# A graph network over a dense 2708 x 2708 matrix: later adj passes and the W2 product by seven products in place of eight

## The chip, the cores and the metric

The kernel runs on 1 core of one Trainium2 chip. The metric is device time in microseconds, the median of several runs, lower is better. TensorE multiplies, VectorE (DVE), ScalarE (ACT) and GpSimd (POOL) work on tiles, SyncE (SP) issues DMAs.

## The reference

x is 2708 x 512, adj 2708 x 2708 (about 2% of its entries are not zero, but it is treated as dense), W1 512 x 1024, W2 1024 x 1024, W3 1024 x 512, all float32. The inputs are drawn in the test; the function is

```python
def _gc(x, adj, W, b):
    return adj @ (x @ W) + b
h = jnp.maximum(_layernorm(x, axis=-1), 0.0)
h = jax.nn.relu(_gc(h, adj, W1, b1))
h = jax.nn.relu(_gc(h, adj, W2, b2))
return x + _gc(h, adj, W3, b3)
```

(the last three lines are `_L0_gnn_ref`, here written into one). The layer norm has eps 1e-5 and no weights.

## The kernel before, in words

**Order of the products.** The kernel forms adj times a matrix in four passes, each with 512 columns of the matrix as stationary operand: `pass1` = adj (normed x); `h1a`, `h1b` = the two halves of relu(pass1 W1 + b1), each followed by its pass, `pass2a` and `pass2b`; `w2` = relu(W2 product + b2); `w3` = its product with W3; `pass3` = adj (that) + b3 + x. 2708 = 21 blocks of 128 and a tail of 20.

**Float32 in three.** Each operand is cut in two fp32r parts, hi (ACT, L530, a CAST) and lo = value - hi (DVE, L551, a subtraction with two SBUF inputs), and `three` (L867 to L869) multiplies hi hi, hi lo and lo hi into one PSUM bank. The tail of 20 rows lies three times in one tile of 84 partitions and needs one matmul (L891).

**A pass.** The 2708 columns go in six chunks of 4, 4, 4, 4, 3 and 2 blocks (512, 384 and 276 wide). For each chunk 21 tiles of adj, 128 x width, are loaded (L419, `raw`, RAW = 7 buffers), cut into a ring (`slot_hi`, `slot_lo`, RING = 7), and each is the moving operand of 4 banks x 3 matmuls. The stationary operand, `still_hi` and `still_lo` of 21 x 512, stays in SBUF. Results are drained by DVE (L806, L816, L813 in pass 3) into `P1` in SBUF or into `stage` (STAGES = 4), and ACT issues their stores (L652 for the output), waiting for DVE's drain. `P2` and `H2` are in DRAM. In all 8352 matmuls: 5920 of 512 columns, 1216 of 384 and 1216 of 276, by the loops.

**The first chunk of pass 1.** Beside each adj tile comes a tile of x (`stage`, loaded by L402 after the tile four before it is cut). DVE takes its statistics two tiles ahead (L712, L714), POOL computes with columns of 128 x 1 (L833 to L847), ACT takes the root and centres (L673, L678) and writes hi (L506), DVE lo (L543). DVE's order for tile n is `statistics(n + 2)`, `inverse(n + 1)` (L719), the cut of the adj tile, the cut of the x tile.

**Order of waits.** Every engine has one list of steps. A load waits until the `raw` buffer's last tile is cut by DVE; a cut by ACT waits for the load and for the ring slot's last matmul; TensorE waits for DVE's `lo_done`. POOL has no work after the x tiles. SP only loads.

## Time and profile before

| what | us |
|---|---|
| median of 3 runs (1734.08 to 1735.21) | 1734.35 |
| the profiled execution: span | 1732.1 |
| TensorE busy (99%), 8352 matmuls | 1717.0 |
| DVE busy (36%) | 628.4 |
| ACT busy (26%) | 451.6 |
| POOL busy (3%) | 43.8 |
| moved by DMA | 190.17 MB, 110 GB/s |

The span runs from the first to the last instruction of one execution; the difference to the median is what lies around it. Matmuls are pipelined: a busy TensorE is one that always has a matmul in it, and the mean of one (0.39 us at 512 columns) is longer than the step from one start to the next. The granted clock was at full speed (2.4 GHz) in all forty slices of the page.

### The profile page before, as it was taken

The page shows a single profiled execution, that of the slowest core. Times are in us where ns is not written, and L with a number is a line of the kernel's source. Part 1 is how long each engine was busy: PE and PEld are TensorE (multiplying, and loading weights), DVE is VectorE, ACT ScalarE, POOL GpSimd, SP SyncE. Part 2 cuts the span into 40 slices and gives each one's busy share as a digit, 9 for nine tenths or more (in the row PEclk, how much of TensorE's full clock was granted, in tenths as well). Part 3 has the DMA queues.
Part 4 walks back from the last instruction along what each step waited for, and adds up shares of the span by engine and source line. Part 5 has one row for each costly group of instructions (what it writes and reads, how often), then busy time and mean ns, then how long its engine had stood idle before and what let it go on. Part 6 is the DMA issues. An engine that isn't in the chain of part 4 may idle for free.

```text
span 1732.1 us, 23105 instructions
## 1 busy us (share of the span) xinstructions
PE 1717.0 (99%) x8352; PEld 1480.0 (85%) x8352; DVE 628.4 (36%) x1040; ACT 451.6 (26%) x829; POOL 43.8 (3%) x115
## 2 busy tenths in 40 slices
PE   7999999999999999999999999999999999999999
PEld 6788889988888899888888899888898888888899
DVE  7623333463332333653233353222233332333232
ACT  6522222332221222332222242111012322222221
POOL 6400000000000000000000000000000000000000
PEclk9999999999999999999999999999999999999999
DMA  5633333024443342133344365332253324444342
GB/s 187 190 94 102 97 97 83 9 62 119 124 116 105 107 128 70 32 105 113 108 121 120 100 188 146 95 96 85 84 154 106 98 87 136 143 147 122 105 123 86
DMA packets 133485, 190.17 MB, mean 110 GB/s; under 512 B 14938, under 2 KB 64698, under 8 KB 133422
## 3 DMA queue, kind: packets, MB, share of 16 engines
q1 hardware_dynamic: 99450, 161.39, 32.5%
q10 hardware_dynamic: 33972, 27.98, 4.9%
q8 instruction: 34, 0.56, 0.1%
q14 instruction: 29, 0.24, 0.0%
HBM read 161.34 MB, written 27.73 MB: 109 GB/s over the span
## 4 chain that ended last, share of the span: by engine, by line
PE 96%; DMA 1%; DVE 1%; POOL 1%; ACT 1%; issue 0%; ACTq 0%; DVEq 0%; SPq 0%
PE ps L867 32%; PE ps L868 32%; PE ps L869 32%; DMA stage<-x 1%; PE ps L891 1%; DVE stats L712 0%; DVE still_lo L543 0%; POOL spread L835 0%; POOL spread L833 0%; POOL spread L843 0%; DVE slot_lo L551 0%; ACT stage L678 0%; ACT still_hi L506 0%; ACT slot_hi L530 0%; DVE moments L714 0%
## 5 line engine op out<-in xcount | busy, mean ns | idle before, releaser
L867 PE MATMUL ps<-slot_hi,still_hi 128*128 128x512 f32 (+2 forms) x2016 | 735.1, 365 | 11.4 <-DVE still_lo L543 11.4
L868 PE MATMUL ps<-slot_lo,still_hi 128*128 128x512 f32 (+2 forms) x2016 | 734.3, 364 | 0.0
L869 PE MATMUL ps<-slot_hi,still_lo 128*128 128x512 f32 (+2 forms) x2016 | 734.0, 364 | 0.0
L551 DVE TENSOR_TENSOR slot_lo<-raw,slot_hi 128x512 fp32r<-128x512 f32 (+2 forms) x588 | 362.8, 631 | 752.0 <-ACT slot_hi L530 751.5
L530 ACT CAST slot_hi<-raw 128x512 fp32r<-128x512 f32 (+2 forms) x588 | 328.5, 573 | 1056.5 <-PE ps L869 784.1
L867 PEld LDWEIGHTS ps<-slot_hi,still_hi 128*128 128x128 f32 x2016 | 379.8, 188 | 65.4 <-DVE still_lo L543 12.4
L868 PEld LDWEIGHTS ps<-slot_lo,still_hi 128*128 128x128 f32 x2016 | 379.9, 188 | 53.0
L869 PEld LDWEIGHTS ps<-slot_hi,still_lo 128*128 128x128 f32 x2016 | 379.6, 188 | 53.1
L867 PE MATMUL ps<-W_hi,slot_hi 128*128 128x512 f32 x336 | 132.1, 393 | 0.0
L868 PE MATMUL ps<-W_lo,slot_hi 128*128 128x512 f32 x336 | 132.1, 393 | 0.0
L869 PE MATMUL ps<-W_hi,slot_lo 128*128 128x512 f32 x336 | 132.1, 393 | 0.0
L867 PE MATMUL ps<-slot_hi,W_hi 128*128 128x512 f32 (+2 forms) x336 | 122.1, 363 | 0.0
L868 PE MATMUL ps<-slot_lo,W_hi 128*128 128x512 f32 (+2 forms) x336 | 121.9, 363 | 0.0
L869 PE MATMUL ps<-slot_hi,W_lo 128*128 128x512 f32 (+2 forms) x336 | 121.9, 363 | 0.0
L868 PEld LDWEIGHTS ps<-W_lo,slot_hi 128*128 128x128 f32 x336 | 63.3, 188 | 14.0
L869 PEld LDWEIGHTS ps<-W_hi,slot_lo 128*128 128x128 f32 x336 | 63.3, 188 | 14.0
L867 PEld LDWEIGHTS ps<-W_hi,slot_hi 128*128 128x128 f32 x336 | 63.3, 188 | 13.7
L868 PEld LDWEIGHTS ps<-slot_lo,W_hi 128*128 128x128 f32 x336 | 63.1, 188 | 8.8
L869 PEld LDWEIGHTS ps<-slot_hi,W_lo 128*128 128x128 f32 x336 | 63.1, 188 | 8.7
L867 PEld LDWEIGHTS ps<-slot_hi,W_hi 128*128 128x128 f32 x336 | 63.1, 188 | 8.7
L808 DVE TENSOR_SCALAR stage<-ps,b_cols 128x512 f32<-128x512 f32 (+2 forms) x48 | 32.7, 687 | 76.9 <-PE ps L869 72.8
L816 DVE COPY stage<-ps 128x512 f32<-128x512 f32 (+2 forms) x48 | 30.1, 628 | 60.0 <-PE ps L891 60.0
(63 smaller groups left out, 563.4 us busy)
## 6 DMA issues: line engine op xcount, KB each, us to landing
raw<-adjT SPq DMA_DIRECT2D x336, 256.0 KB, 2.7
raw<-adjT SPq DMA_DIRECT2D x84, 192.0 KB, 2.4
raw<-adjT SPq DMA_DIRECT2D x84, 138.0 KB, 2.1
raw<-H SPq DMA_DIRECT2D x42, 256.0 KB, 2.9
raw<-W SPq DMA_DIRECT2D x32, 256.0 KB, 3.1
P<-stage ACTq DMA_DIRECT2D x32, 256.0 KB, 2.1
raw<-P SPq DMA_DIRECT2D x32, 256.0 KB, 2.7
H<-stage ACTq DMA_DIRECT2D x32, 256.0 KB, 2.3
```

What stands on the lines that cost most here:

```text
L530: act.copy(hi, src).then_inc(hi_done, 1)
L551: dve.tensor_tensor(lo, src, hi.bitcast(F32), ALU.subtract).then_inc(lo_done, 1)
L808: dve.tensor_scalar(stage[:, d.stage, 0:w], ps[:, d.bank, 0:w], b2_cols[:, d.part:d.part + 1], 0.0, ALU.add, ALU.max).then_inc(drained, 1)
L816: dve.tensor_copy(stage[:, d.stage, 0:w], ps[:, d.bank, 0:w]).then_inc(drained, 1)
L867: pe.matmul(out, st_hi, mv_hi, start=start, stop=False)
L868: pe.matmul(out, st_hi, mv_lo, start=False, stop=False)
L869: return pe.matmul(out, st_lo, mv_hi, start=False, stop=stop)
L891: return pe.matmul(out, still_tail[0:REP, b * P:(b + 1) * P], slot_tail[0:REP, 0:w], start=False, stop=True)
```

## The change

**Seven products.** In `pass2a`, `pass2b`, `pass3` and `w2` the operands are seen as 2 x 2 blocks: adj by pairs of row blocks (t, t + 10), t = 0 to 9, and by two halves of 1356 columns (adj's columns are padded from 2708 to NP = 2712); the stationary operand by the same pairs and by two halves of its 512 columns. Seven products X_i Y_i take the place of eight: three of blocks as they are, four of sums and differences. Row block 20 and the tail are added directly, to the groups of parts 1, None, 5 and 6. Each half goes in CHUNKS = 3 chunks of W = 452 columns. A group is one part of one chunk: 10 tiles of adj (or of its combinations), each for 2 banks x 3 matmuls; in `w2` 4 tiles, each for 4 banks x 3. Its drain adds it to partial results in SBUF (`parts`, `e(i)`); part 4 is added in two places.

**The combinations of adj** are made once, in pass 1, by POOL (`make`: four subtractions of 452 columns for each pair and chunk) from the loaded tiles, and stored to `TS`, from which the later passes load. Those of the stationary operands are made in `combine` (POOL, for pass 2a and pass 3) or in `prep_stationary` (POOL, from `H1B` and `W2` in DRAM, with DMAs issued by POOL), stored, and loaded and cut anew in groups 2, 3, 5, 6 and 7 of the last chunk of pass 2a and pass 2b (ten or eight tiles of 128 x 256 among the ten moving tiles) and in the first two groups that follow. `prep_moving` does the same for the moving operand of `w2`.

**Pass 1** stays direct, but with 3 chunks of 2 x 452 columns, eight banks and adj tiles of 904 columns, RAW1 = 5, RING1 = 3. x tiles have XS = 3 buffers. The results `P1` go to DRAM. W1 is done in one phase `h1` with both halves; its first half stays in SBUF, the second (`H1B`) goes to DRAM.

**Stores.** ACT issued them after waiting for the drain. Now SP does, in its stream of loads: the store of parts 1, 4, 5 and 6 stands two tiles behind the drain (`later(2, store)`; four in pass 3), the drain LAG = 5 tiles behind its group. RAW and RING are 5. In pass 3 POOL adds x (`finish`), with its own loads of `xT`.

```diff
-RING = 7
-RAW = 7
-HEAD = 4
-LATE = 4
-STAGES = 4
...
-CHUNK_BLOCKS = (4, 4, 4, 4, 3, 2)
...
+ORDER = (1, 2, 3, 4, 5, 6, 0, 7, 8, 9)
+EARLY = 8
+BLOCKS = [b for t in ORDER for b in (t, t + PAIRS)] + [20, SHORT]
...
+W = 452
+CHUNKS = 3
+HALF = W * CHUNKS
+NP = 2 * HALF
...
+DIRECT = {0: (0, 0), 1: (1, 0), 6: (1, 1)}
+X11, X12, S2, S3, S1, X22, S4 = range(7)
+
+RING = 5
+RAW = 5
+RAW1 = 5
+RING1 = 3
+XS = 3
+LAG = 5
...
+    def adj_pass(name, late, reload=None, ahead=(), own=()):
+        last_of = {}
+        ahead, own = list(ahead), list(own)
+        for c in range(CHUNKS):
+            for g_n, part in enumerate((0, 1, 2, 3, None, 4, 5, 6)):
...
+                half = {1: 0, None: 1, 5: 0, 6: 1}.get(part)
+                for t in here + ([20] if half is not None else []):
+                    if t == 20:
+                        j = p.tile("left", True)
+                        j.chunk, j.half = c, half
+                        g.left = j
+                        p.release(j, g, True)
...
+                    if half is not None and (t == here[0] if here else True):
+                        p.tails += 1
+                        g.tail = (p.tails, c, half, at["tail_freed"])
+                        at["tail_freed"] = g.done[-1]
+                        p.steps.append(("tail", g))
+                    spread_in(extra)
+                    if late:
+                        late.pop(0)()
+                    if own and c == 0 and g_n == 0 and len(g.tiles) > RING + 1:
+                        own.pop(0)()
+                    p.emit_due()
...
+                p.later(LAG, lambda g=g: drain_product(g))
...
+    def drain_product(g):
+        part = g.part
+        count_drains(g, (0, 1), 2 if part == 4 else 1)
+        finals = {1: ("c11", 4), 4: ("c22", 6), 5: ("y", 2), 6: ("x", 0)}.get(part)
+        needs = {0: 0, 1: 4, 3: 2, None: 6}.get(part)
+        busy = [p.busy(("e", needs + m)) for m in range(2)] if needs is not None else [None, None]
+        p.steps.append(("drain", (g, p.copied if part == 0 else p.drained, busy)))
+        if finals:
+            p.owed |= {("e", finals[1] + m) for m in range(2)}
+            def store():
+                for m in range(2):
+                    p.store(("e", finals[1] + m))
+                p.steps.append(("store", (g, finals, g.free_drained)))
+                if g.phase != "pass3":
+                    at["p2", g.phase, g.chunk] = dict(p.stored)
+            if g.phase == "pass3":
+                p.final += 2
+                p.final_of[g.chunk, g.part] = p.final
+                p.steps.append(("finish", (g, finals, g.free_drained, p.final)))
+                p.later(4, store)
+            else:
+                p.later(2, store)
...
+                if n >= XS:
+                    sp.wait_ge(lo1_done, xs1[n - XS].ready)
+                sp.dma_start(xs[:, n % XS, :], x[b * P:(b + 1) * P, :]).then_inc(x_in[n % XS], 16)
...
+                elif j.kind == "moving" and j.part in DIRECT:
+                    k, a = DIRECT[j.part]
+                    b = j.pair + k * PAIRS
+                    col = a * HALF + j.chunk * W
+                    sp.dma_start(raw[:, r, 0:W], adjT[b * P:(b + 1) * P, col:col + W]).then_inc(raw_in[r], 16)
+                elif j.kind == "moving":
+                    if "made" not in seen:
+                        seen["made"] = 1
+                        for i in range(2):
+                            sp.wait_ge(made_stored[i], 16 * made_total // 2)
+                    k = (j.part - 2) * W
+                    sp.dma_start(raw[:, r, 0:W], TS[j.pair, j.chunk, :, k:k + W]).then_inc(raw_in[r], 16)
...
+                elif kind == "store":
+                    g, finals, number = a
+                    half = 0 if g.part in (1, 5) else 1
+                    side = 0 if g.part in (1, 6) else 1
+                    col = half * HALF + g.chunk * W
+                    if g.phase == "pass3":
+                        sp.wait_ge(finished, plan.final_of[g.chunk, g.part])
+                    else:
+                        sp.wait_ge(drained, number)
...
+                elif kind == "tail":
+                    n = a.tail[0]
+                    act.wait_ge(tail_in, 48 * n)
+                    act.wait_ge(group_done, a.tail[3])
+                    act.copy(slot_tail[0:REP, 0, :], raw_tail[0:REP, 0, :]).then_inc(tail_hi, 1)
...
+            def make(i, which):
+                c, n = divmod(i, PAIRS)
+                a, b = chunks1[c][2 * n], chunks1[c][2 * n + 1]
+                upper, lower = raw1[:, a.raw % RAW1, :], raw1[:, b.raw % RAW1, :]
+                Y11, Y12, Y21, Y22 = upper[:, 0:W], upper[:, W:2 * W], lower[:, 0:W], lower[:, W:2 * W]
+                T2_, T3_, T1_, T4_ = (made[:, i % 2, k, :] for k in range(4))
+                if which == 0:
+                    if i >= 2:
+                        pool.wait_ge(made_stored[i % 2], 16 * (i // 2))
+                    pool.wait_ge(raw1_in[a.raw % RAW1], 16 * (a.raw // RAW1 + 1))
+                    pool.tensor_tensor(T1_, Y12, Y11, ALU.subtract).then_inc(made_done, 1)
+                    pool.wait_ge(raw1_in[b.raw % RAW1], 16 * (b.raw // RAW1 + 1))
+                    pool.tensor_tensor(T3_, Y22, Y12, ALU.subtract).then_inc(made_done, 1)
+                else:
+                    pool.wait_ge(made_done, 4 * i + 1)
+                    pool.tensor_tensor(T2_, Y22, T1_, ALU.subtract).then_inc(made_done, 1)
+                    pool.wait_ge(made_done, 4 * i + 3)
+                    pool.tensor_tensor(T4_, Y21, T2_, ALU.subtract).then_inc(made_done, 1)
+
...
+            def prep_moving(c, q):
+                cols = [slice(a * HALF + c * W, a * HALF + (c + 1) * W) for a in range(2)]
+                y11, y12, y21, y22 = (prep[:, i, 0:W] for i in range(4))
+                for i, (k, a) in enumerate(((q, 0), (q, 1), (KF + q, 0), (KF + q, 1))):
+                    prep_load(i, P2[k, :, cols[a]], prep[:, i, 0:W])
+                n = state["done"]
+                state["done"] += 4
+                pool.wait_ge(prep_in[0], state["in"][0])
+                pool.wait_ge(prep_in[1], state["in"][1])
+                pool.tensor_tensor(y11, y12, y11, ALU.subtract).then_inc(prep_done, 1)
+                pool.wait_ge(prep_in[3], state["in"][3])
+                pool.tensor_tensor(y12, y22, y12, ALU.subtract).then_inc(prep_done, 1)
+                pool.wait_ge(prep_done, n + 2)
+                prep_store(0, T2[0, q, c, :, :], y11)
+                prep_store(1, T2[1, q, c, :, :], y12)
+                pool.tensor_tensor(y22, y22, y11, ALU.subtract).then_inc(prep_done, 1)
+                pool.wait_ge(prep_in[2], state["in"][2])
+                pool.wait_ge(prep_done, n + 3)
+                pool.tensor_tensor(y21, y21, y22, ALU.subtract).then_inc(prep_done, 1)
+                pool.wait_ge(prep_done, n + 4)
+                prep_store(2, T2[2, q, c, :, :], y22)
+                prep_store(3, T2[3, q, c, :, :], y21)
...
+            def product_group(g):
+                first = g.chunk == 0 and g.phase in ("pass2a", "pass3")
+                phase = "h1" if g.phase == "pass2a" else "w3"
+                side = 0 if g.part in (0, 1, 6) else 1
+                for n, j in enumerate(g.tiles):
+                    if first:
+                        pe.wait_ge(stat_lo, plan.stat_of[phase, j.pair, j.part])
+                    pe.wait_ge(lo_done, j.cut + 1)
+                    s = j.slot % RING
+                    for m in range(2):
+                        cols = slice(m * P, (m + 1) * P)
+                        if n == 0:
+                            bank_free(g, m)
+                        end = g.left is None and n == len(g.tiles) - 1
+                        mm = three(ps[:, g.banks[m], 0:W], S[:, j.pair, j.part, 0, cols], S[:, j.pair, j.part, 1, cols],
+                                   ring[:, s, 0, 0:W], ring[:, s, 1, 0:W], start=n == 0, stop=end)
+                        if end:
+                            mm.then_inc(group_done, 1)
+                    if not end:
+                        mm.then_inc(slot_used, 1)
```

## Rows read from the trace of the kernel before

**Rows 1.** The profile's page: busy time by engine; below, the chain by line.

```profile
PE 1717.0 (99%) x8352; PEld 1480.0 (85%) x8352; DVE 628.4 (36%) x1040; ACT 451.6 (26%) x829; POOL 43.8 (3%) x115
...
PE ps L867 32%; PE ps L868 32%; PE ps L869 32%; DMA stage<-x 1%; PE ps L891 1%; DVE stats L712 0%; DVE still_lo L543 0%; POOL spread L835 0%; POOL spread L833 0%; POOL spread L843 0%; DVE slot_lo L551 0%; ACT stage L678 0%; ACT still_hi L50
```

**Rows 2.** Waits of TensorE: us in total, times, longest.

```profile
PE ps L867 <- DVE still_lo L543: 11.4, 3, 9.5
```

**Rows 3.** Timeline of TensorE, 512 columns: start, us, operation; 18 rows left out.

```profile
399.63 0.39 PE L869 MATMUL ps<-slot_hi,still_lo 128*128 128x512 f32 x1
...
403.93 0.39 PE L867 MATMUL ps<-slot_hi,still_hi 128*128 128x512 f32 x1
```

**Rows 4.** The same, 384 columns; 12 rows left out.

```profile
254.71 0.33 PE L869 MATMUL ps<-slot_hi,still_lo 128*128 128x384 f32 x1
...
256.96 0.33 PE L867 MATMUL ps<-slot_hi,still_hi 128*128 128x384 f32 x1
```

**Rows 5.** The same, 276 columns; 14 rows left out.

```profile
299.83 0.29 PE L867 MATMUL ps<-slot_hi,still_hi 128*128 128x276 f32 x1
...
301.76 0.29 PE L867 MATMUL ps<-slot_hi,still_hi 128*128 128x276 f32 x1
```

**Rows 6.** Groups by line and form: count, busy us, mean ns of one, idle before.

```profile
L551 DVE TENSOR_TENSOR slot_lo<-raw,slot_hi 128x512 fp32r<-128x512 f32 x406 | 273.2, 689 | 545.5 <-ACT slot_hi L530 545.2 <-DVE still_tail L745 0.2
L530 ACT CAST slot_hi<-raw 128x512 fp32r<-128x512 f32 x406 | 244.8, 620 | 740.7 <-PE ps L869 561.4 <-DVE stage L808 67.2 <-DVE stage L816 65.6
...
L551 DVE TENSOR_TENSOR slot_lo<-raw,slot_hi 128x276 fp32r<-128x276 f32 x91 | 39.6, 445 | 94.3 <-ACT slot_hi L530 94.3
L530 ACT CAST slot_hi<-raw 128x276 fp32r<-128x276 f32 x91 | 37.6, 423 | 140.3 <-PE ps L869 100.0 <-DVE stage L808 17.4 <-DVE stage L816 15.1
```

**Rows 7.** Timeline of the first 11 us, all engines.

```profile
0.73 0.53 POOL L850 MEMSET slot_tail<- 128x512 f32 x1 [0.29 <-POOLq L1035]
...
5.74 0.34 POOL L843 TENSOR_SCALAR spread<-spread 128x1 f32<-128x1 f32 x1 [0.54 <-DVE spread L719]
...
9.53 0.79 PE L867 MATMUL ps<-slot_hi,still_hi 128*128 128x512 f32 x1 [9.53 <-DVE still_lo L543]
...
9.87 0.43 SPq L419 DMA_DIRECT2D raw<-adjT  x1
...
10.12 0.63 PE L868 MATMUL ps<-slot_lo,still_hi 128*128 128x512 f32 x1
...
10.54 0.63 PE L869 MATMUL ps<-slot_hi,still_lo 128*128 128x512 f32 x1
```

**Rows 8.** The chain of waits from 38 to 62 us: start, us, what.

```profile
46.66 2.65 DMA stage<-x
...
49.34 0.70 DVE stats L712
...
50.06 0.19 DVE moments L714
...
61.08 1.37 POOL spread L843
```

**Rows 9.** Timeline around 46 us, DVE and POOL.

```profile
42.52 0.13 DVE L719 RECIPROCAL spread<-spread 128x1 f32<-128x1 f32 x1
...
45.88 0.75 DVE L543 SCALAR_TENSOR_TENSOR still_lo<-stage,spread,still_hi 128x512 fp32r<-128x512 f32 x1 [0.15 <-ACT still_hi L506]
...
46.07 0.77 POOL L843 TENSOR_SCALAR spread<-spread 128x1 f32<-128x1 f32 x1
```

**Rows 10.** DMA issues: count, KB each, median us from issue to landing.

```profile
raw<-adjT SPq DMA_DIRECT2D x336, 256.0 KB, 2.7
...
raw<-adjT SPq DMA_DIRECT2D x84, 138.0 KB, 2.1
```

**Rows 11.** One stretch of 2 us: PE, PEld, DVE, ACT, POOL busy, clock, DMA share, GB/s.

```profile
1000.00:1002.00 2.00, 2.00 (x14) 2.00 (x13) 1.44 (x3) 1.51 (x3) 0.00 (x0) 1.00 1.06 396
```

**Rows 12.** Timeline of the last matmul.

```profile
1728.96 0.29 PE L891 MATMUL ps<-slot_tail,still_tail 84*128 84x276 f32 x1
```

More of the change, by code:

```diff
@@ L37 @@
 BANK = 512
[L38 to L67 removed]
+EPS = 1e-5
+STEP = 32
+PAIRS = 10
+FULL = 21
+SHORT = 21
+ORDER = (1, 2, 3, 4, 5, 6, 0, 7, 8, 9)
+EARLY = 8
@@ new lines, with __init__ @@
+BLOCKS = [b for t in ORDER for b in (t, t + PAIRS)] + [20, SHORT]
[11 more added lines that the diff above has]
+LAG = 5
+class Tile:
+    def __init__(self, kind, cut):
+        self.kind, self.cut = kind, cut
+        self.raw = self.raw_freed = self.slot = None
+        self.block = self.part = self.pair = self.chunk = self.half = self.k = None
+        self.freed = self.place_freed = None
@@ L68, in __init__, with columns_chunk @@
+def columns_chunk(block):
+    first = block * P
+    last = min(first + P, 2 * HALF) - 1
+    return max((c % HALF) // W for c in range(first, last + 1))
+class Pass1Tile:
+    def __init__(self, kind, cut):
         self.kind, self.cut, self.ready = kind, cut, cut + 1
-        self.chunk, self.tile, self.col, self.width, self.half, self.source = chunk, tile, col, width, half, source
-        self.raw = self.raw_freed = self.tail_use = self.slot = self.acc_before = self.slot_before = None
+        self.raw = self.raw_freed = self.pair_freed = self.slot = None
+        self.freed = self.place_freed = None
+        self.chunk = self.block = self.n = self.k = self.col = None
@@ L367, in source_of @@
[L367 to L383 removed]
+        copied = sem("copied")
@@ L818, in finish @@
-            def finish(dve, g, i):
-                if g[0].phase != "w3":
-                    still_lo_part(g, len(g[0].drains) - 1, i)
-                    dve.wait_ge(still_done, count([u.drains[-1].still for u in g], i))
-            run_cuts_and_drains(dve, cut, drain, finish, drain_first=("h1a", "h1b"))
+                    elif n + 2 <= SHORT:
+                        statistics(n + 2)
+                    if n + 1 <= SHORT:
+                        inverse(n + 1)
+                dve.wait_ge(hi1_done, j.cut + 1)
@@ new lines, in w2_group @@
+            def w2_group(g):
+                for n, j in enumerate(g.tiles):
+                    pe.wait_ge(lo_done, j.cut + 1)
+                    s = j.slot % RING
+                    for m in range(4):
+                        half, mm_col = divmod(m, 2)
+                        cols = slice(mm_col * P, (mm_col + 1) * P)
+                        if n == 0:
+                            bank_free(g, m)
+                        t = 2 * j.pair + half
+                        mm = three(ps[:, g.banks[m], 0:W], S[:, t, j.part, 0, cols], S[:, t, j.part, 1, cols],
+                                   ring[:, s, 0, 0:W], ring[:, s, 1, 0:W], start=n == 0, stop=n == 3)
+                        if n == 3:
+                            mm.then_inc(group_done, 1)
+                    if n < 3:
+                        mm.then_inc(slot_used, 1)
```

1857 lines of the change are left out of this document (1138 added, 719 removed).

## The prediction

> **What bounds the kernel now.** I read the busy times first: TensorE 1717.0 of 1732.1 us, and 32% of the chain that ended last for each of the three lines of `three`, 96% in all [rows 1]. The waits of TensorE come next: 11.4 us on its first line, of which 9.53 are the start [rows 2, 7]. So nothing but the stream of matmuls sets the end, and time is gained by fewer or narrower ones. The timeline gives the price of one, start to start. 512 columns: 19 steps from 399.63 to 403.93, 0.2263 us [rows 3]. 384: 13 steps from 254.71 to 256.96, 0.1731 [rows 4]. 276: 15 steps from 299.83 to 301.76, 0.1287 [rows 5]. Each is its columns at 2.4 GHz plus 13 to 14 ns, so 452 columns cost 188.3 + 13.2 = 0.2015 us. That is the one price I interpolate, and three points lie on the line.
>
> Check on before: 5920 matmuls of 512, 1216 of 384 and 1216 of 276 (8352, the page's count) make 1339.7 + 210.5 + 156.5 = 1706.7 us. From first to last matmul the trace has 1729.25 - 9.53 = 1719.7 [rows 7, 12]. Of the 13.0 left, 2.3 are the slow first dozen at 0.42 apart [rows 7], 1.9 the other waits on that line [rows 2], and 8.8 (0.5%) are spread.
>
> **The change part by part.**
>
> **Matmuls.** The two-by-two split takes seven products where eight were. Pass 1 stays direct: 3 chunks x 8 banks x 64 = 1536 matmuls. Each of the three later passes has 3 x (7 parts x 10 pairs x 2 x 3 + 4 x 2 x 4 for block 20 and the tail) = 1356. W2 has 3 x 7 x 4 x 4 x 3 = 1008. That makes 6612 of 452 columns, 1332.3 us. The two block phases keep 528 each of 512, 239.0 us. Together 1571.3, or 135.4 less than before. With 0.5% spread (8.0) and the slow start (2.3): 1581.6.
>
> **Ends.** The first matmul needs a cut of 904 columns instead of 512. A DVE cut costs 0.689 at 512 and 0.445 at 276 [rows 6], so 1.04 ns a column: 0.63 at 452, 1.10 at 904 and 0.42 at 256. ACT's goes from 0.620 and 0.423 [rows 6] to 0.57, 0.95 and 0.41. So 9.53 becomes 10.3. At the end, 1732.1 - 1729.25 = 2.9 us of drain and store [rows 12] become two drains in a row, two additions on POOL and the store: about 5.6. Sum: 1597.5.
>
> **Seams, where one phase takes the banks or buffers of another.** Pass 1 to W1: the last bank is copied (0.63), then ACT cuts the first block (0.62) and DVE (0.69), with handovers: 2.2. W1 to pass 2a: only two moving tiles are cut when the short block ends (2.4 us of matmuls). Before the third, DVE and ACT do a stationary cut (0.41 and 0.42), two drains (1.4), a relu and two more stationary cuts, so it is ready after 5.2: 2.8 lost. W3 to pass 3, likewise: 1.4. Sum: 1603.9.
>
> **Chunk 0 of pass 1, the largest stall.** The x tiles now have XS = 3 buffers where STAGES = 4 were. DVE does `statistics(n + 2)` at the head of tile n, so x tile n + 2 must be there, and SyncE loads it only when tile n - 1 is cut. Each tile then holds a whole load in series. The chain before shows what that is: the x cut ends at 46.63 [rows 9], the load takes 2.65 from 46.66 and the statistics start at 49.34, so 2.71 in all, then 0.70, then 0.19 [rows 8]. Add the reciprocal 0.13 [rows 9], the wide cut 1.10, the x cut 0.75 [rows 9] and handovers: 5.7 a tile. The matmuls of a tile take 24 x 0.2015 = 4.84. In the kernel before a tile of slack lay between, and TensorE's tile hid it.
> POOL also gets four subtractions of 452 columns a pair (`make`). No row has a two-input POOL operation of any width. From below, its memset of 512 took 0.53 [rows 7], so 0.47 at 452; from above, its longest operation took 1.37 [rows 8]. I take 0.9, between them. A POOL operation and a DVE operation with two SBUF inputs don't overlap: the POOL line that takes 0.34 alone [rows 7] took 0.77 when it began 0.19 after a DVE cut, and ended 0.2 after that had ended [rows 9]. Before, only POOL paid for that; with operations of 0.9, DVE pays too, part of one for a tile, 0.2. So 5.9 a tile, 19 times, from 10.3 to 122.4; the last cuts (3.7) and the last tile (6.45) follow: 132.6, against 115.8 at matmul speed. Lost: 17 (13 without the lock, 28 if each tile waits for half of a POOL operation).
> The Trainium skill has this as a rule (SBUF — State Buffer, two separate sides): the shared port pair is an exclusive lock, held for a whole instruction by whoever starts first. The trace agrees. Its GPSIMD Engine Reference (Performance versus the Vector engine) gives 4497 ns for 2048 elements; an estimate from it is 0.99 us at 452, and the stall would be about 1 us more.
>
> **Tails.** The `tail` step of a group stands behind its first tile and waits for the tail's last user. For part 6 that is part 5, the group just before, so ACT stands still until TensorE has finished part 5 with one tile (1.21) in hand. The next is ready after 2.0: 0.8 lost, 9 times: 7.
>
> **SyncE's queue.** A store stands in the loads two cuts behind its drain, and SyncE waits there for the drain; behind it are the loads of all five raw buffers. In a pass a tile lasts 6 x 0.2015 = 1.21. The load that would go out 2.4 before cut D ends goes out after the drain (1.3) and two issues of 0.43 [rows 7], 2.2 after it. A load of 226 KB lands in 2.6, between 2.1 for 138 and 2.7 for 256 [rows 10]; with ACT and DVE it is usable at 6.3, at 7.7 if the two stores go first on the wires. TensorE wants it at 7.1. So parts 1 and 6 lose 0 to 0.6. Part 4 has four drain operations, 1.3 more: 0.4 to 1.8. Part 5, after the tail stall, loses 0.6 to 1.9. Over nine chunks this is 9 to 44. I take 9, since the loads are cheap while the wires are half used: they carried 396 GB/s in one stretch of 2 us [rows 11], and a pass asks for 191 in loads and 20 in stores. If this cover goes, it is 44. What it takes off ACT (about 50 issues of 0.43) hides behind matmuls in both kernels and is worth nothing.
>
> **Reloads.** In the last chunk of passes 2a and 2b and the first of 2b, 10 (or 8) stationary tiles go through the same five buffers in a group. A buffer's round is a load (2.31, the mean of 226 and 128 KB by [rows 10]), ACT 0.49, DVE 0.53 and handovers 0.15 to 0.3: 3.5 to 3.65, so 0.70 to 0.73 a cut and 14.0 to 14.6 for 20 cuts, where the matmuls take 12.1 (13.7 with block 20). With a lead of 3.5 us eaten first, 4 to 10 us over the five groups in a row and the two; 27 without any lead, 0 if loads overlap better. I take 6.
>
> **What is put at nothing:** POOL's preparation in passes 2a and 2b (18 stationary pairs, 12 moving ones). It has 180 us for some 9 us x 18, and its issue on POOL is in no row: from below an issue of SyncE, 0.43 [rows 7]; from above a landing, 2.7 [rows 10]. Near the lower, it fits. Without cover SyncE waits for `prep_out`; for loads and lock beside it up to 15. The W2 drains (2 to 4 operations in a group of 9.7 us) have a tile to spare.
>
> Sum: 1603.9 + 17 + 7 + 9 + 6 = 1642.9 span. The median of before is 2.25 over its profiled span, so 1645.
>
> **The rivals.**
> (a) *Matmul-bound but for the seams:* the x loads and store waits vanish in lead that I don't see. 1603.9 + 2.25 = 1606, up to 1620 with a part of chunk 0. For it: 99% busy now [rows 1]. Against: the chain of [rows 8] already has the load in it.
> (b) *The load stream paces the passes:* 44 + 27 + 15 instead of 9 + 6: about 1716 in full, 1690 in the middle. For it: the moving preparation asks 142 GB/s (1.85 MB in some 13 us) on top of 211; against: 396 was seen [rows 11]. The Trainium skill (DMA: Bandwidth & Descriptors, Specifications) states some 358 GB/s of HBM for a core; by it those 353 would just fill it. The row of 396 is over that, in a burst.
> (c) *Slower than before:* landings under POOL's traffic outlast the five raw buffers all through. A pass tile turns from 1.21 to T when landing exceeds 5T - 1.3, which is 4.8 now. To lose the remaining 90 us over 666 tiles needs T = 1.35 and a landing of 5.4 us, twice the 2.7 of [rows 10]. At 5.6 us it is 1760. Against: no group of loads lands near that.
> (d) *The split saves less:* if 452 columns cost as 512, 6612 x 0.025 = 164 more. The three widths on one line [rows 3 to 5] speak against it.
>
> **How the numbers follow.** Forecast 1645: chance 0.52, own range 1620 to 1672. (a) 0.14. (b) 0.26. (c) 0.06, with (d) in it. Within 0.2% (3.5 us, about what a measurement of this kernel can tell) 0.02. Faster: 0.52 + 0.14 + 0.26 = 0.92. Range 1608 to 1698: nearly all of the forecast, most of (a), and (b) but for its far end.
>
> **What would show it.** After: 7668 matmuls; starts 0.20 apart at 452; in the first 130 us TensorE about 82% busy with one wait of about 1 us a tile on the x cut, and DVE waiting for `x` loads; TensorE waits near 0.8 at part 6 and at groups with reloads; SyncE waiting for drains at its stores. The forecast is wrong if TensorE is over 98% busy (a), or if its waits in plain chunks exceed 5 us a chunk with ACT waiting for raw loads (b, c).

## The result and the profile after

The changed kernel took 1868.15 us (median of 4 runs, 1862.55 to 1870.98), the kernel before 1734.78 beside it. The ratio is 1.0766 with a 95% interval of 1.0744 to 1.0789: 7.7% slower, where 1645 (1608 to 1698) was forecast. The profiled execution has a span of 1868.9, 226 over the 1642.9 of the sum.

The page of after: busy times, the slices that tell of clock and wires, the chain by engine, and the price of the DMA issues (KB each, median us from issue to landing).

```profile
PE 1693.2 (91%) x7668; PEld 1475.0 (79%) x7668; DVE 994.4 (53%) x1581; ACT 753.9 (40%) x1428; POOL 531.0 (28%) x651
...
PEclk9999999999999899989999988999999999899998
...
DMA packets 229686, 366.18 MB, mean 196 GB/s; under 512 B 26000, under 2 KB 207464, under 8 KB 229572
...
PE 32%; DMA 16%; DVE 10%; ACT 3%; issue 2%; POOL 1%; SPq 0%; ACTq 0%; POOLq 0%; DVEq 0%
...
raw<-TS SPq DMA_DIRECT2D x360, 226.0 KB, 3.3
raw<-adjT SPq DMA_DIRECT2D x306, 226.0 KB, 3.4
```

The 7668 matmuls are the ones that were counted. But TensorE, 99% busy before [rows 1], is 91% busy, and DMA has entered the chain. Of the 226 us, half is idle time of TensorE (1868.9 - 1693.2 = 175.7, where the sum had 61). The other half is busy time (1693.2 against 1581.6): the same matmuls took longer.

Who waited for whom in after (us in total, times, longest), first of the engines, then of SyncE's queue:

```profile
ACT ring L951 <- DMA raw<-TS: 201.3, 146, 8.1
ACT ring L951 <- DMA raw<-adjT: 167.2, 113, 8.2
...
PE ps L1425 <- DVE ring L1113: 124.6, 85, 5.2
...
PE ps L1425 <- DVE still L1076: 27.6, 15, 10.8
```

```profile
SPq L867 <- POOL parts L1419: 75.8, 12, 13.4
SPq L851 <- ACT parts L1031: 75.0, 17, 7.7
...
SPq L851 <- ACT spill L1031: 48.3, 6, 10.5
...
SPq L867 <- DVE parts L1234: 41.0, 12, 7.1
```

In before, all waits of TensorE on this line were 11.4, the start among them [rows 2]. Now it waits 124.6 for the ring cuts, 85 times; DVE waits for ACT, and ACT for loads from HBM, although the wires carry 196 GB/s on average, half of the 396 seen in before [rows 11]. That points at loads that were sent late, and the second fence names a sender: SyncE stands in front of stores for 163.9 us in all on L867 (the passes, two more lines of the view counted) and 123.3 on L851 (W2). Whether that is the cause is for the experiments to show.

One such stretch of pass 3, the timeline of after without TensorE (start, us, engine, line):

```profile
1659.49 3.76 SPq L774 DMA_DIRECT2D raw<-TS  x4
...
1664.48 1.28 DVE L1212 SCALAR_TENSOR_TENSOR parts<-ps,b_cols,parts 128x452 f32<-128x452 f32 x2
...
1665.84 2.97 POOL L1419 TENSOR_TENSOR parts<-parts,prep 128x452 f32<-128x452 f32 x2 [27.10 <-DVE parts L1212]
...
1668.76 1.09 POOL L1410 DMA_DIRECT2D prep<-xT  x2
1668.84 0.81 SPq L867 DMA_DIRECT2D outT<-parts  x2
1669.70 8.39 SPq L774 DMA_DIRECT2D raw<-TS  x8
1675.18 0.57 ACT L951 CAST ring<-raw 128x452 fp32r<-128x452 f32 x1 [6.31 <-DMA raw<-TS]
```

The same stretch in windows of 2 us (the last three columns are the granted clock of TensorE, DMA share and GB/s):

```profile
1666.00:1668.00 2.00, 2.00 (x11) 1.83 (x10) 1.88 (x3) 0.95 (x2) 2.00 (x2) 1.00 0.00 0
...
1672.00:1674.00 2.00, 2.00 (x11) 1.83 (x10) 0.00 (x0) 0.00 (x0) 0.00 (x0) 1.00 0.93 324
1674.00:1676.00 2.00, 0.40 (x2) 0.02 (x1) 0.22 (x1) 0.65 (x2) 0.00 (x0) 1.00 0.96 340
1676.00:1678.00 2.00, 1.53 (x5) 1.38 (x6) 1.89 (x4) 1.98 (x4) 0.00 (x0) 0.69 0.41 127
1678.00:1680.00 2.00, 2.00 (x7) 1.76 (x6) 1.31 (x3) 0.79 (x2) 0.00 (x0) 0.50 0.87 285
```

The two drains end at 1665.76, POOL's two additions of 1.5 us each follow, and only at 1668.84 does SyncE send the stores. It has sent no load since 1663.3. For two microseconds nothing moves at all. Then two stores, two `xT` loads of POOL (sent once the same additions are done) and five `raw` loads go out within 3.5 us, the other loads of that row later, as buffers come free. The first load, sent at 1669.70, is there at 1675.16: 5.46 us, where one took 2.7 in before [rows 10]. Not every store has such a landing behind it. The loads sent behind a store of pass 2b and behind the one above (KB each, median us to landing):

```profile
raw<-TS SPq DMA_DIRECT2D x3, 226.0 KB, 3.2
...
raw<-TS SPq DMA_DIRECT2D x5, 226.0 KB, 5.8
```

Behind the stores of pass 3 the first load took 5.0 to 6.5 us, behind those of passes 2a and 2b 2.8 to 5.1, 3.0 on the median. TensorE has eaten the ring by then and stands for 2.07 us. And then it is slow. TensorE in after, behind this stall:

```profile
1676.47 0.52 PE L1425 MATMUL ps<-ring,S 128*128 128x452 f32 x1 [2.07 <-DVE ring L1113]
1676.78 0.58 PE L1426 MATMUL ps<-ring,S 128*128 128x452 f32 x1
...
1680.17 0.38 PE L1426 MATMUL ps<-ring,S 128*128 128x452 f32 x1
1680.39 0.37 PE L1427 MATMUL ps<-ring,S 128*128 128x452 f32 x1
```

From 1676.78 to 1680.17 there are nine steps of 0.377, which is 452 columns at 1.2 GHz, the lower level; the window shows a granted clock of 0.50. Each stall of over 2 us in pass 3 but one is followed by 7 to 15 such steps, 0.17 too long each: 1.2 to 2.6 us on top of the stall. Over the whole of after, 307 steps are over 0.33 us, and together they are 54 us too long.

### The profile page after: what moved, and what is told of

It is laid out like the page before. It is cut to its first block, busy times and chain, and to the rows that moved or that the text cites. A ratio compares the mean times of both kernels' runs of the same rounds, so it can differ in the third digit from the quotient of the medians.

```text
span 1868.9 us, 22422 instructions
## 1 busy us (share of the span) xinstructions
PE 1693.2 (91%) x7668; PEld 1475.0 (79%) x7668; DVE 994.4 (53%) x1581; ACT 753.9 (40%) x1428; POOL 531.0 (28%) x651
## 4 chain that ended last, share of the span: by engine, by line
PE 32%; DMA 16%; DVE 10%; ACT 3%; issue 2%; POOL 1%; SPq 0%; ACTq 0%; POOLq 0%; DVEq 0%
PE ps L1425 11%; PE ps L1426 10%; PE ps L1427 10%; DMA raw<-TS 7%; DVE ring L1113 7%; DMA raw<-adjT 6%; ACT ring L951 2%; DVE S L1113 1%; DMA raw<-W2S 1%; DMA raw<-S2B 1%; POOL parts L1419 1%; DMA raw<-W 1%; DMA raw<-T 1%; PE ps L1530 0%; DMA raw<-H1B 0%
## 5 line engine op out<-in xcount | busy, mean ns | idle before, releaser
L1113 DVE TENSOR_TENSOR ring<-raw,ring 128x452 fp32r<-128x452 f32 (+1 forms) x816 | 567.4, 715 | 484.8 <-ACT ring L951 479.3
L1425 PE MATMUL ps<-ring,S 128*128 128x452 f32 x1596 | 618.3, 387 | 125.7 <-DVE ring L1113 120.3
L951 ACT CAST ring<-raw 128x452 fp32r<-128x452 f32 (+1 forms) x816 | 460.9, 572 | 622.8 <-DMA raw<-TS 201.3
L1426 PE MATMUL ps<-ring,S 128*128 128x452 f32 x1596 | 604.8, 379 | 0.0
L1427 PE MATMUL ps<-ring,S 128*128 128x452 f32 x1596 | 603.7, 378 | 0.0
L1425 PEld LDWEIGHTS ps<-ring,S 128*128 128x128 f32 x1596 | 311.4, 195 | 198.6 <-DVE ring L1113 128.2
L1427 PEld LDWEIGHTS ps<-ring,S 128*128 128x128 f32 x1596 | 311.3, 195 | 32.1
L1426 PEld LDWEIGHTS ps<-ring,S 128*128 128x128 f32 x1596 | 312.3, 196 | 29.4
L1425 PE MATMUL ps<-slots,still 128*128 128x452 f32 x504 | 190.3, 378 | 31.7 <-DVE still L1076 27.6
L1426 PE MATMUL ps<-slots,still 128*128 128x452 f32 x504 | 187.4, 372 | 0.0
L1427 PE MATMUL ps<-slots,still 128*128 128x452 f32 x504 | 186.8, 371 | 0.0
L1091 DVE TENSOR_TENSOR slots<-raw,slots 128x904 fp32r<-128x904 f32 x63 | 82.1, 1305 | 128.0 <-ACT slots L920 128.0
L1425 PEld LDWEIGHTS ps<-slots,still 128*128 128x128 f32 x504 | 96.5, 192 | 47.4 <-DVE still L1076 33.8
L920 ACT CAST slots<-raw 128x904 fp32r<-128x904 f32 x63 | 59.2, 943 | 147.5 <-PE ps L1427 139.1
L1427 PEld LDWEIGHTS ps<-slots,still 128*128 128x128 f32 x504 | 96.4, 191 | 9.3
L1426 PEld LDWEIGHTS ps<-slots,still 128*128 128x128 f32 x504 | 96.7, 192 | 7.9
L1113 DVE TENSOR_TENSOR S<-raw,S 128x256 fp32r<-128x256 f32 x126 | 58.4, 465 | 26.4 <-ACT S L951 25.3
L1425 PE MATMUL ps<-W1c,ring 128*128 128x512 f32 x176 | 68.5, 389 | 2.7 <-DVE ring L1113 2.7
```

Of the source, the lines that this page charges most:

```text
L920: act.copy(slots1[:, j.slot % RING1, 0, :], raw1[:, j.raw % RAW1, :]).then_inc(hi1_done, 1)
L951: act.copy(hi, src).then_inc(hi_done, 1)
L1091: dve.tensor_tensor(slots1[:, s, 1, :], raw1[:, j.raw % RAW1, :], slots1[:, s, 0, :].bitcast(F32), ALU.subtract).then_inc(lo1_done, 1)
L1113: dve.tensor_tensor(lo, src, hi.bitcast(F32), ALU.subtract).then_inc(lo_done, 1)
L1425: pe.matmul(out, st_hi, mv_hi, start=start, stop=False)
L1426: pe.matmul(out, st_hi, mv_lo, start=False, stop=False)
```

## Experiments

Three explanations fit these rows: SyncE's wait at the stores lets the buffers run dry; the stores, sent by the same engine, go out ahead of the loads; or the loads land late by the pass's own traffic, whoever waits. The expectations, each written before its run, name them by letters.

**Stores on ACT, as before.** The one edit takes the store steps out of SP's list and puts them into ACT's, word for word otherwise.

```diff
-                elif kind == "store":
-                    g, finals, number = a
...
-                        sp.wait_ge(drained, number)
...
-                        sp.dma_start(dst, e(finals[1] + m)).then_inc(e_stored[finals[1] + m], 16)
+                elif kind == "store":
+                    g, finals, number = a
...
+                        act.wait_ge(drained, number)
...
+                        act.dma_start(dst, e(finals[1] + m)).then_inc(e_stored[finals[1] + m], 16)
```

> Edit: the changed kernel, with the stores of finished results (passes 2a, 2b, 3 and W2) issued by ACT at the same place in its own list of steps, as before the change, and not by SyncE. Theory W (SyncE waits for the drain in front of its loads; this wait empties the five raw buffers, TensorE stands still 2 to 4 us after a store and then runs some microseconds at half clock): most of that goes, some 37 places at 2.5 us of waiting and 1.5 us of clock, so about 1720 us (1690 to 1750) against 1868. Rival L (226 KB loads land in 3.3 us where 2.6 were expected, and five raw buffers are too few for that, wherever the stores are): nearly the same, 1840 to 1870. Rival F (the wait is harmless, but the two stores stand ahead of the loads in SyncE's rings): about 1720 too.

Measured: 1768.49 (1765.55 to 1771.92), 1.0202 of before (1.0182 to 1.0221), so 100 us less than after: two thirds of the way to the 1720 of the explanations that blame SyncE, and far from the 1840 to 1870 of the one that blames the traffic. Its span is 1765.1; TensorE is busy for 1655.0 and idle for 110, so of 104 us 66 were idle time and 38 busy time, nearly all of it slow steps (54 us of them in after, 19 here). The waits and 100 us of pass 3, first of this kernel, then the same clock times of after, which also lie in its pass 3:

```profile
PE ps L1425 <- DVE ring L1113: 64.8, 73, 5.2
...
1600.00:1700.00 100.00, 99.21 (x480) 89.53 (x479) 65.66 (x100) 46.44 (x85) 16.57 (x16) 1.00 0.76 233
```

```profile
1600.00:1700.00 100.00, 85.97 (x377) 76.24 (x376) 52.22 (x79) 38.17 (x70) 12.04 (x12) 0.91 0.64 191
```

480 matmuls against 377 in the same time. Pass 3, whose loads come from the same tensors with the same buffers, is nearly without loss once SyncE does not wait. It moves more bytes, not fewer, so the wires were not what held it. What ACT pays for the 114 issues that it took over doesn't show.

Long landings are not what held it either, so long as SyncE goes on. In this kernel too stores and `xT` loads go out together in pass 3, and the loads beside them land no sooner:

```profile
raw<-TS SPq DMA_DIRECT2D x4, 226.0 KB, 5.5
```

Here the first load behind such a pair took 4.3 to 6.5 us, with no wait of SyncE for a result, and TensorE hardly stopped. Counted from the first matmul of a phase to that of the next, after is longer by 27 us in pass 2a, 16 in pass 2b, 9 in W2 and 51 in pass 3: 2.3, 1.3 and 4.3 us for each of the twelve store places of a pass.

**Stores on SyncE, but later.** Is it the wait, or that the stores are on the same queue?

```diff
-                p.later(4, store)
+                p.later(9, store)
             else:
-                p.later(2, store)
+                p.later(7, store)
```

> Edit: the stores stay with SyncE, but stand seven cuts behind the drain in place of two (nine in place of four in pass 3), so that SyncE, which is five cuts ahead of DVE, comes to them when the drain is over. The bytes and their place in SyncE's rings ahead of the next loads stay. Theory W (the wait): as with ACT's stores, about 1720 us, within 15 us of that run. Rival F (stores ahead of loads in the rings): 1830 to 1870. Rival L (landing of loads): 1840 to 1870.

Measured: 1782.69 (1776.81 to 1788.78), 1.0268 (1.0244 to 1.0293). SyncE's waits at L867, 163.9 us in after, are down to 11.7 (those of W2, 122, stayed, since those steps weren't moved). 85 of the 100 us come back with the same stores on the same queue. So the wait is what costs; the order on the queue is worth at most the other 15, with W2's waits in them.

**Four x buffers.**

```diff
-XS = 3
+XS = 4
```

> Edit: four buffers for the x tiles in pass 1 in place of three, nothing else. Theory X (each tile of the first chunk waits for the load of the x tile that the buffer of the tile before frees): the waits of TensorE on the x cut, 27.6 us in all, of which 10.8 is the start, go to a few us: 15 to 20 us less, some 1850 us. Rival P (the first chunk is held by POOL's subtractions and the port that it shares with DVE's cuts): under 5 us less.

Measured: 1843.72 (1837.63 to 1848.21), 1.064 (1.062 to 1.066): 24 less than after. TensorE's wait for the x cut falls from 27.6 (15 times) to this, which is the start and one more:

```profile
PE ps L1424 <- DVE still L1075: 11.1, 2, 10.8
```

So 16.5 us of waits went, and pass 1 as a whole became 22.7 us shorter (349.7 to 327.0). Of the 6 beyond the waits only 1 is steps at the lower clock; most of the rest lies at the edges of the 13 stalls that went: the first step after a wait takes 0.31 instead of 0.205, and the last matmul before one counts as busy to its end. The theory named what happened; its 15 to 20 us left the edges out.

**All of it together:** stores on ACT, XS = 4, and seven raw buffers, paid for with a ring slot.

```diff
-RING = 5
-RAW = 5
+RING = 4
+RAW = 7
...
-XS = 3
-LAG = 5
+XS = 4
+LAG = 4
```

> Edit: stores by ACT, four x buffers, and seven raw buffers in place of five, paid for by four ring slots in place of five (drains then stand one cut earlier). Theory W + X + R (the raw buffers are what is too few, because a load lands in 3.3 us; the ring's slots are not): 1640 to 1670 us, so under the kernel before the change by 4%. Rival S (with four slots the cuts are late instead, since a cut takes 1.3 us after a slot is free): 1700 or more.

Measured: 1697.97 (1695.56 to 1702.75), 0.9791 of before (0.9768 to 0.9815): with the stores back on ACT and the buffers dealt otherwise, the seven products make the kernel 2.1% faster than before. Less what stores and x buffers gave, 1768.49 - 24 - 1697.97 leaves 46 for the two raw buffers, if the parts add up. The 1640 to 1670 of the expectation was missed. The rival's reason for that, that four ring slots make the cuts late, is not what the phases show: a chunk of pass 3 takes 94.5 us, and its 452 matmuls at 0.2067 make 93.4. What is over lies in the last chunks of passes 2a and 2b, where reloads stand among the tiles: 105 and 114 us (116 and 125 with stores on ACT alone). In the rows of this kernel the tail stall stands by itself, four times at exactly this length and once at 0.88:

```profile
849.20 0.47 PE L1423 MATMUL ps<-ring,S 128*128 128x452 f32 x1 [0.79 <-DVE ring L1111]
```

**Seven raw buffers alone.** If the loss at a store is that five buffers run dry, two more should cover it.

```diff
-RING = 5
-RAW = 5
+RING = 4
+RAW = 7
...
-LAG = 5
+LAG = 4
```

> The changed kernel with its stores still on SyncE, and seven raw buffers instead of five, paid for with one ring slot (4 for 5; the drain lag is 4 tiles and the W2 drains stand a tile or two earlier). Theory: SyncE's wait costs what it does because five raw buffers are less than the wait plus a landing of 5.5 to 6.5 us. Two more buffers are 2.4 us of cover, about the length of one stall (2.1 to 4.4 us), so most of the 100 us of the waits go as well as the 46 that the buffers gave with the stores on ACT: 1740 to 1780, with the stalls behind stores under 1 us. Rival A: buffers and waits are separate costs, so only the 46 goes: 1822, with stalls behind stores as long as now. Rival B: seven loads that go out together land later than five did, which takes back the cover: over 1822, and landings above 7 us behind a store.

Measured: 1861.33 (1854.97 to 1869.77), 1.0751 (1.0709 to 1.0792): only 7 us less than after. Theory and rival A both fell, and rival B's landings above 7 us did not come (5.2 to 6.1 behind the stores of pass 3). The waits of TensorE are in sum those of after, and SyncE waits longer, not shorter, in front of the same stores (163.9 in after; here, with two more lines of the view, 286):

```profile
PE ps L1424 <- DVE ring L1112: 123.6, 63, 5.2
```

```profile
SPq L866 <- POOL parts L1418: 118.8, 12, 15.9
...
SPq L866 <- DVE parts L1233: 85.1, 12, 10.0
```

One store of this kernel in SyncE's timeline:

```profile
1573.68 6.03 SPq L766 DMA_DIRECT2D raw<-adjT  x7
1591.15 0.82 SPq L866 DMA_DIRECT2D outT<-parts  x2
```

SyncE had sent its last load at 1579.7 and stood for 11.4 us. With more buffers it comes to the store sooner, and waits there for the same event. What lies ready when it is let go is the number of tiles that the store stands behind the drain (two or four), plus the ring, whatever RAW is; here the ring had one slot less. This makes a new theory, which needs a test of its own. Pass 3 fits it: it became 17 us longer than in after (340.0 to 356.7), and a slot less of 1.24 us at twelve stores makes 15. Passes 2a and 2b do not fit it as it stands: they became 17 and 7 us shorter, so that there the two buffers gave something in spite of the store. The 7 us are the sum of the two.

**Seven raw buffers, four x buffers and stores on SyncE seven tiles behind the drain.**

```diff
-                p.later(4, store)
+                p.later(9, store)
             else:
-                p.later(2, store)
+                p.later(7, store)
```

(with the edits of RING, RAW, LAG and XS from above)

> The changed kernel with its stores on SyncE, four x buffers, seven raw buffers (four ring slots), and the stores of the passes seven tiles behind the drain instead of two (nine instead of four in pass 3). New theory, after seven buffers alone moved the time by 7 us: what is loaded ahead when SyncE is let go is the number of tiles that the store stands behind the drain, whatever the number of raw buffers, since SyncE only reaches the store sooner with more of them. Then seven tiles behind the drain with seven buffers leaves no wait in the passes, and the two buffers give their 46 us again: within 15 us of the version with stores on ACT (1697.97), so 1698 to 1720, the rest being the W2 and block-phase stores, which stay where they are. Rival: the wires are what the two buffers of the ACT version relieved only together with ACT's issue, so that seven buffers give 7 us here too: 1782.69 - 24 - 7 = 1752.

Measured: 1707.26 (1702.45 to 1709.85), 0.9843 (0.9821 to 0.9866), within 10 us of the version with stores on ACT. The rival's 1752 is out. The two buffers are worth 7 us with the store two tiles behind the drain and about 50 with it seven behind (1782.69 - 24 - 1707.26 = 51, if the parts add up). By phase, from its first matmul to that of the next, in us:

| | pass 1 | pass 2a | pass 2b | W2 | pass 3 |
|---|---|---|---|---|---|
| after | 349.7 | 352.8 | 343.6 | 220.9 | 340.0 |
| stores on ACT | 347.5 | 325.7 | 327.8 | 212.2 | 288.7 |
| seven raw buffers alone | 346.4 | 335.5 | 336.2 | 217.1 | 356.7 |
| all, stores on ACT | 326.4 | 303.8 | 306.3 | 208.3 | 288.6 |
| all, stores on SyncE seven tiles behind | 325.7 | 303.1 | 308.0 | 216.8 | 288.6 |

The last two rows are alike but for W2, whose stores were not moved. Distances between two and seven tiles were not run. One store of pass 3 in this kernel, in SyncE's timeline, has less than a microsecond in front:

```profile
1440.80 0.32 SPq L772 DMA_DIRECT2D raw<-TS  x1
1441.82 0.81 SPq L865 DMA_DIRECT2D outT<-parts  x2
1442.68 6.37 SPq L772 DMA_DIRECT2D raw<-TS  x7
```

**The price of a column.** In after, the steps at 452 are 0.2067 apart in the later passes and W2, against my 0.2015:

```profile
1672.17 0.37 PE L1427 MATMUL ps<-ring,S 128*128 128x452 f32 x1
...
1674.03 0.37 PE L1427 MATMUL ps<-ring,S 128*128 128x452 f32 x1
```

Nine steps in 1.86. In pass 1 they are 0.2042 to 0.2050, and at 512 they are 0.2267. Is it the width, or the way the operands lie? In this kernel the later passes and W2 leave out the last four columns of each chunk.

```diff
-                        mm = three(ps[:, g.banks[m], 0:W], S[:, j.pair, j.part, 0, cols], S[:, j.pair, j.part, 1, cols],
-                                   ring[:, s, 0, 0:W], ring[:, s, 1, 0:W], start=n == 0, stop=end)
+                        mm = three(ps[:, g.banks[m], 0:448], S[:, j.pair, j.part, 0, cols], S[:, j.pair, j.part, 1, cols],
+                                   ring[:, s, 0, 0:448], ring[:, s, 1, 0:448], start=n == 0, stop=end)
```

> The version with stores on ACT, four x buffers and seven raw buffers, with the matmuls of passes 2a, 2b, 3 and of W2 made 448 columns wide instead of 452; the last four columns of each chunk are left out. Theory A: something in how 452 columns lie costs (the width is no multiple of 64, or rows of 1808 bytes): then the step from one matmul to the next falls from 0.2067 to 448 at 2.4 GHz plus 13 ns, 0.2000, and the run by 5076 x 0.0067 = 34 us to about 1664. Theory B: the layout of the stationary tile or the alternation of products costs some 5 ns a matmul whatever the width: 0.205, and 1689.

Measured: 1690.65 in one run, which theory B's 1689 meets. Its TensorE, first in W2, then in pass 3:

```profile
1159.89 0.37 PE L1424 MATMUL ps<-ring,S 128*128 128x448 f32 x1
...
1164.85 0.37 PE L1424 MATMUL ps<-ring,S 128*128 128x448 f32 x1
...
1599.79 0.37 PE L1425 MATMUL ps<-ring,S 128*128 128x448 f32 x1
...
1603.84 0.37 PE L1424 MATMUL ps<-ring,S 128*128 128x448 f32 x1
```

In pass 3, twenty steps in 4.05 are 0.2025: between A's 0.2000 and B's 0.205. Over the columns at 2.4 GHz that is 15.8 ns, where 452 has 18.4 in this layout and about 16 in pass 1, and 512 has 13. But in W2, and in the first stretch of each later pass, the steps are 0.2067 (24 in 4.96 above), which is what 452 columns cost there. The width and the stationary tile are the same in both places. Of all undisturbed steps of this operand the mean is 0.2046 (0.2067 at 452), which is why the time meets B's number; its reason, one excess whatever else, fails as A's does. What makes the 5 ns stays open.

**Tail and reloads smoothed.** The best version, with two more edits: the tail's step at the sixth tile of its group, and the reloads dealt over more groups.

```diff
-                    if half is not None and (t == here[0] if here else True):
+                    if half is not None and (t == here[5] if here else True):
...
-                if reload and c == CHUNKS - 1 and part is not None and part >= 2:
-                    extra = reload(part - 2, last_of)
+                if reload and c == CHUNKS - 1:
+                    if part is not None and part >= 2:
+                        if part < 6:
+                            kept += reload(part - 2, last_of)
+                    here_n = {2: 7, 3: 8, None: 2, 4: 8, 5: 8, 6: 11}.get(part, 0)
+                    extra, kept = kept[:here_n], kept[here_n:]
```

> The version with stores on ACT, four x buffers and seven raw buffers (1697.97), with two more edits: the tail step stands at the sixth tile of its group instead of the first, and the reloads of the stationary tiles are spread more evenly (parts 4 to 6 are reloaded in the pass that follows, up to eleven in a group elsewhere). Theory: the 0.79 us stalls are the tail's wait for the group before (9 x 0.8 = 7 us) and some 25 us are reload groups whose loads outrun the buffers; with both smoothed TensorE is about 98% busy: 1660 to 1680. Rival: the reload groups are limited by all of a pass's traffic, so that the stall only moves to the following pass: 1685 to 1700, with the 0.79 waits gone and as much waiting at the first groups of passes 2b and 3.

Measured: 1684.92 (1682.78 to 1687.23), 0.9716 (0.9699 to 0.9733). That is 13 under the version before it, and 2.8% faster than the kernel before; it is short of the 1660 to 1680 expected. The stalls of 0.79 are gone; in pass 3 three of 0.40 to 0.49 are left in their place. In the last chunk of pass 2a the waits of 6.6 us became 3.6. In that of pass 2b, where the reloads for W2 stand beside the last moving tiles, 13.1 us in 11 waits became 10.0 in 15 (0.2 to 1.4 us each). The first groups of passes 2b and 3 did not wait more than before; that of W2 now waits 2.4, where it had no wait. So neither text is right as it stands: little moved, but a part of the reloads is still limited.

```profile
PE 1627.3 (97%) x7668; PEld 1444.7 (86%) x7668; DVE 1001.8 (59%) x1581; ACT 756.3 (45%) x1428; POOL 544.4 (32%) x651
...
PE ps L1432 <- DVE ring L1120: 28.5, 31, 5.2
```

## Why the prediction was wrong

By its own steps, with what each term measured. "Idle" is TensorE's.

| step of the sum | taken | measured |
|---|---|---|
| matmuls counted | 7668 | 7668 |
| price at 452 | 0.2015 | 0.2067 and about 0.205: some 31 us more |
| start | 10.3 | 10.8 (10.1 to 11.2 in the other runs) |
| seams | 2.2, 2.8, 1.4 | 2.65, 5.15, 2.38 |
| x chain of chunk 0 | 17 (13 to 28) | 24 by the fourth buffer, of which 16.5 waits |
| tails | 0.8 each, nine times | 0.79 each, where they stand by themselves |
| SyncE's queue | 9 (9 to 44) | 100: 66 idle, and the rest mostly slow steps |
| reloads, five raw buffers | 6 (0 to 27) | with stores on ACT 52 over two plain chunks in the last chunks of 2a and 2b alone; with seven buffers still 30. All of what two buffers gave: 46 |
| lower clock behind stalls | not there | 54 us of slow steps in after, 14 in the version with all of it together; most of it also in the rows above |

**The step that failed is SyncE's queue.** Its mechanism was the right one and its place too: SyncE waits two cuts behind a drain and the loads stand behind it. Its working goes wrong in one number above all: "A load of 226 KB lands in 2.6". In pass 2b that nearly holds (2.8 to 4.0 behind its stores), and there the step cost 16 us, near the 14.7 of the step's upper end for one pass. In pass 2a the first load behind a store took up to 5.1, and the cost was 27. In pass 3 it took 5.0 to 6.5, and the cost was 51. Put into the step, the 5.46 of the store above turns "usable at 6.3" into 9.2 against the 7.1 at which TensorE wants it, 2 us lost at a plain store and 3.4 at part 4; the stalls behind the stores of pass 3 measured 1.9 to 4.4. Pass 3 has another thing that the step left out: the store there waits for POOL's two additions too, 2.97 us, and the two extra tiles of `later(4)` (2.4 us) don't cover them. The 36 store places of the passes cost 2.6 us on average, 94 in all where the upper end was 44, and about a third of it is slow steps, which the step had not counted. The stores of W2, which it did not price, cost 9 more. (What it took off ACT was 114 issues, not about 50; nothing hangs on that.)

Why a load lands so late in pass 3 is only partly shown. It is not the row of loads that the wait itself has made: in pass 2b a row of five behind two stores landed in 3.0 to 4.3, and in pass 3 it is as long with stores on ACT. What stands beside it in pass 3 and not in pass 2b are POOL's two `xT` loads, sent at the same moment; a kernel without them was not run.

The cheapness that I gave as the reason for the lower end, "the wires are half used", is true of the mean (196 GB/s) and says nothing of the moment: in the windows above they carry 0 and then 340. The Trainium skill (DMA: Bandwidth & Descriptors, Specifications) states some 358 GB/s for a core, by which rival (b) was weighed; the 340 of the burst is near it, and the mean is far from it. What came near that limit was a burst of a few us.

**What the sum didn't have at all is the clock.** I took every wait at its length. Behind most waits of over 2 us, and some shorter ones, the granted clock went from 1.00 to 0.50 for some microseconds, and the steps from 0.207 to 0.377. It did not behind all: the wait of 2.36 at 1560 us has none. The rows of before show the lower level only at the start, as the slow first dozen [rows 7]; the sum priced them there and nowhere else. Behind the three waits of 0.79 in after it was one to three such steps.

**The price at 452** was called a point on a line through three others. Three widths on one line did not carry to a fourth: 0.2067 instead of 0.2015, 31 us. Rival (d), 452 at the price of 512, is out.

**x chain:** the mechanism was right and the number somewhat low. From one `xs` load to the next there were 7.15 and 5.38 us, 6.2 on the average, where I had 5.9. POOL's subtractions are the mis-sized part: 1.16 us each on the median (its additions 1.5 in pass 3, beside DVE), where I took 0.9 and the estimate from the Trainium skill's page on GpSimd (GPSIMD Engine Reference, Performance versus the Vector engine) was 0.99. The wide DVE cut took 1.305 on average, against 1.10. 43 of the 63 are at 1.08 to 1.2; the other 20, up to 2.09, all ran beside a two-input operation of POOL.

```profile
L1091 DVE TENSOR_TENSOR slots<-raw,slots 128x904 fp32r<-128x904 f32 x63 | 82.1, 1305 | 128.0 <-ACT slots L920 128.0
...
L1419 POOL TENSOR_TENSOR parts<-parts,prep 128x452 f32<-128x452 f32 x24 | 35.6, 1505 | 271.2 <-DVE parts L1226 118.0
```

**Reloads and buffers:** with stores out of the way, five buffers still cost 46 us against seven. A load lands in 3.3 to 3.8 on the median, not 2.3 to 2.6, in kernels that move 366 MB where before moved 190. I priced too few buffers for the reload groups alone, and too low there. A chunk of pass 2a without reloads took 104 with stores on ACT and 95.5 with seven buffers; beside it runs POOL's preparation, which the sum put at nothing. No run takes that preparation away. Two of the three seams lost about 1 to 2.4 us more than counted; the size of the first was right within half a microsecond.

**The rivals.** The time that came is beyond rival (c), slower, at 0.06, and its reason is not the one that is shown. It wanted a landing of 5.4 all through; measured were 3.3 to 3.4 on the median, and 5.0 to 6.5 only behind the stores of pass 3, where with stores on ACT landings as long cost nothing. Rival (b), the load stream paces the passes (1716), holds for the chunks with reloads; the plain chunks of pass 3 run at the pace of TensorE once the stores are out of SyncE's way (94.5 us against 93.4 of matmuls). Rival (a) is out with TensorE 91% busy. My sign of a wrong forecast, waits over 5 us a chunk with ACT waiting for raw loads, was the right one to look for: the stalls of a chunk in pass 3 sum up to 12 to 13 us.

## What to carry over

A DMA issue that waits for a result, put into an in-order queue of loads, must stand so many tiles behind it that the queue does not wait. Seven tiles did it here, for five and for seven buffers; two did not. More load buffers alone bring the queue to the wait sooner (7 us for two of them, against 50 once the distance was seven tiles). Ask what else the same event releases, and price the blocked queue at the landing beside that traffic (5.0 to 6.5 us in pass 3), not at the median of before (2.7); add the matmuls at half clock that follow most stalls of over 2 us. Give saved work its own test apart from the moved issues: the kernel with seven products ended 2.8% faster than before, and the stores' place had cost 100 us.

## What the runs showed of the hardware that I had not expected

- Behind most stalls of over 2 us TensorE ran nine or so matmuls of 452 columns at 0.377 us, which is 452 / 1.2 GHz with nothing over it; at 2.4 GHz the same ones have 18 ns over their columns. Over the whole run the mean granted clock was 0.962 in after, 0.986 with stores on ACT and 0.990 with all of it together.
- 452 columns cost 0.2067 us from start to start where the stationary operand is the seven-part tile, about 0.205 in pass 1. 448 columns of the same operand cost 0.2025 in pass 3 and 0.2067 in W2. 512 columns cost 0.2267 (0.2263 in the rows of before). The cause is open.
- Loads of 226 KB that went out beside two stores and POOL's two `xT` loads in pass 3 landed all late, the first hardly sooner than the rest: 5.46 to 5.9 us for five in after, 5.74 for the first with seven buffers, at up to 340 GB/s. Five behind two stores in pass 2b, without `xT` loads, took 3.0 to 4.3, one after the other.
- A two-input operation of POOL at 128 x 452 took 1.16 us on the median in pass 1 (subtractions) and 1.5 in pass 3 (additions, each beside a cut of DVE).
